# A ViT block of three attentions and a routed feed forward network: half 0 of the data placed ahead of half 1, and the up weights prepared on other engines

## The chip, the cores and the metric

The kernel runs on one core of a Trainium2 chip. The metric is the device time of one execution in microseconds (us); lower is better. The time before is the median of three runs.

A core has five engines that run in parallel, each in order of its own queue: TensorE (PE in the profile; PEld is its loading of weights) multiplies matrices into the eight banks of PSUM, VectorE (DVE) and ScalarE (ACT) compute elementwise from the buffer or from PSUM, GpSimd (POOL) computes elementwise from the buffer alone, and SyncE (SP) issues transfers. They wait for each other on semaphores.

## The reference

The input is 16 images of 3 x 128 x 128. Everything is float32. Cut to what matters here:

```python
h = layer_norm(patches @ conv_w.T + conv_b) + pe           # 16 x 64 tokens, 64 features
identity = h
h = ffn(h)                                                 # gelu, 64 -> 256 -> 64
h = windowed_attention(h) + identity                       # first attention, 8 heads of 8
identity = h
h = ffn(h) + identity                                      # second use of the same ffn: "ffn2"
# second attention: one head of 64, a bias from cosines, inside a block with layer norm
h = layer_norm(h + softmax(q @ k.T / 8 + bias) @ v)
# third: rms norm, rotary q and k, causal attention with 4 heads
x = h + attention(rms_norm(h) * ln1_w) @ wo.T
flat = rms_norm(x) * ln2_w
w = top-2-of-8 softmax(flat @ router_w.T), normalised
y = sum over e of w[e] * (silu(flat @ w1[e].T) * (flat @ w3[e].T)) @ w2[e].T
out = layer_norm(h + x + y)
```

## The kernel before

The 16 images x 64 positions x 64 features lie as 128 partitions x 512 columns (two images' features share the partitions), and nearly every step is done in two halves g = 0 and 1 of 256 columns (`HC`). Each engine's program is one list written out by hand in `build`: the order of the calls is the order of its queue, and semaphores alone tie the engines together. Steps of half 0 and half 1 are interleaved by hand.

What the change touches, in order of time:

- **First attention** (`att1`, L863 and L1269). Eight windows w. TensorE does `scores1(w)`, `turn1(w-1)` (the transpose of the shifted scores), `mix1(w-2)`; VectorE the maximum and the subtraction (`shift`, L1234, L1236); ScalarE the exp (L867). Windows 0 to 3 are half 0. A half ends with `divide` on VectorE (L1245, L1247), `mixed_to_features` on TensorE (two transposes, L426), `attended_copy1` on ScalarE (L861), `project1` on TensorE (L431) and `residual1` on VectorE (L1291), which makes h2.
- **Second feed forward** (`ffn2`): `ffn_up` (L351), two `gelus` on ScalarE (L808), `ffn_down` (L361), `ffn2_out` on VectorE (L1301), which makes h3.
- **Second attention** (`att2`): `queries_keys2` (L500) in two banks that both halves use in turn, q copied by ScalarE (L890), k by VectorE (`keys2`, L1308), `open_scores2` (the bias put in the scores' bank ahead of them, L483), `scores2` (L515), `shift2` on VectorE (L1322, L1324), `turn2` (L506), exp (L896), `values2` (L523 and L1329; the value weights are centred once by `centre_values2`, L1158 and L1165), `mix2` (L536), `divide2` (L1344, L1346), `residual2` (L1351).
- **Root mean square norm**: squares (VectorE L1361 for half 0, ScalarE L903 for half 1), their sums (L1174), ScalarE's square root (L906), reciprocal (L1180) and scaling (L1185) on VectorE, which makes `h4n`; `turn_h4` (L566) and ScalarE's copy `h4f` (L911); then two pairs of products for keys and queries of each half (`turned_pair`, L575), which VectorE rotates (L1375, L1382).
- **The up weights** `up_w` (2816 columns, loaded early) are multiplied by `ln2` and split in a rounded high part `up_hi` and a rest `up_lo`: L1284 and L1296, on VectorE. They are read in the last stage (L707, L708), behind the third attention. `down_w` is centred by GpSimd (L1077 to L1085), which waits for VectorE's key slots (`k1_dve`, L1217) before it starts.

ScalarE has one function table at a time: `bring_table` (L794) loads the next, 1.28 us plus a first use.

## Time and profile before

| | |
|---|---|
| Time, median of 3 runs | 115.91 us (115.75 to 115.92) |
| The profiled execution | 115.73 us, of which its span 113.9 us |
| Mean granted TensorE clock | 0.983 |
| TensorE busy | 100.1 us, 88% |
| VectorE busy | 81.2 us, 71% |
| ScalarE busy | 64.0 us, 56% (nine table loads, 11.5 us) |
| GpSimd busy | 33.3 us, 29% |
| Chain that ended last | TensorE 59%, VectorE 19%, ScalarE 7%, transfers 6% |

The busy shares are averages over stages with different limits. In the first attention (about 21 to 39 us) and in the last stage with the experts' products (73 to 105 us) TensorE is all but full. Between them, from 39 to 72 us, the work passes from engine to engine in two halves, and the chain of waits tells more than the shares. GpSimd's total includes 22.7 us without work, from 32 to 55 us.

### The profile page before, as it was taken

The numbers are of one execution on the slowest core, as the hardware profiler recorded it, in microseconds if no ns is written. First come the engines' busy times: TensorE is split into PE (matmuls) and PEld (weight loads), VectorE is DVE, ScalarE is ACT, GpSimd is POOL, SyncE is SP. The second block draws the span as 40 slices with busy tenths as digits, with TensorE's granted clock in tenths as the row PEclk, the third lists the DMA queues.
The fourth block names the chain that finished last, engine by engine and source line by source line (L and its number), as shares of the span: only waits on it lengthen the run. The fifth ranks groups of instructions, "written<-read, shape, count | busy, mean of one in ns | idle before, by whom it ended". The sixth has DMA issues, their size and how long they took to land.

```text
span 113.9 us, 2196 instructions
## 1 busy us (share of the span) xinstructions
PE 100.1 (88%) x825; PEld 64.5 (57%) x828; DVE 81.2 (71%) x173; ACT 64.0 (56%) x125; POOL 33.3 (29%) x68
## 2 busy tenths in 40 slices
PE   5998979999999998977699887999999999999710
PEld 2334547376676764663568665688888874334400
DVE  0002417597889889889598975589589899976981
ACT  5005364976533754927388657467476667478040
POOL 7500034973830000000622073030012350879000
PEclk9999999999999999999999999999999999999985
DMA  3999994000000000000000000000000000000004
GB/s 125 368 387 419 441 409 172 0 0 0 6 0 0 0 3 6 3 0 0 0 0 6 0 0 6 0 0 0 0 0 6 3 0 0 3 0 0 0 0 92
DMA packets 2826, 6.99 MB, mean 61 GB/s; under 512 B 1280, under 2 KB 1408, under 8 KB 2688
## 3 DMA queue, kind: packets, MB, share of 16 engines
q1 hardware_dynamic: 2272, 6.72, 15.2%
q10 hardware_dynamic: 544, 0.13, 0.5%
q8 instruction: 6, 0.10, 0.4%
q14 instruction: 4, 0.03, 0.1%
HBM read 6.59 MB, written 0.26 MB: 60 GB/s over the span
## 4 chain that ended last, share of the span: by engine, by line
PE 59%; DVE 19%; ACT 7%; DMA 6%; issue 3%; SPq 2%; POOL 1%; DVEq 0%; ACTq 0%
PE PS L707 9%; PE PS L708 9%; PE PS L715 7%; DMA shared_x<-x_dram 6%; PE PS L393 4%; PE PS L351 4%; PE PS L575 3%; PE PS L404 3%; PE PS L361 3%; DVE shifted L1236 2%; DVE top L1234 2%; PE PS L418 2%; ACT shared_f L808 2%; PE PS L327 2%; PE PS L515 1%
## 5 line engine op out<-in xcount | busy, mean ns | idle before, releaser
L707 PE MATMUL PS<-xf,up_hi 128*128 128x512 f32 x44 | 17.8, 405 | 0.2 <-DVE xf L1402 0.2
L1454 DVE TENSOR_TENSOR shared_h<-PS,shared_f 128x512 f32<-128x512 f32 x22 | 15.0, 683 | 3.4 <-ACT shared_f L973 3.1
L708 PE MATMUL PS<-xf,up_lo 128*128 128x512 f32 x44 | 17.3, 394 | 0.0
L973 ACT ACTIVATE shared_f<-PS 128x512 f32<-128x512 f32 x22 | 13.1, 596 | 6.4 <-PE PS L708 6.2
L794 ACT ACT_TABLE_LOAD x9 | 11.5, 1283 | 0.9 <-PEq L1671 0.7
L1234 DVE TENSOR_REDUCE top<-PS 128x8 f32<-128x512 f32 x12 | 8.3, 688 | 3.0 <-PE PS L393 2.7
L707 PEld LDWEIGHTS PS<-xf,up_hi 128*128 128x128 f32 x44 | 8.3, 188 | 2.2 <-issue 0.4
L708 PEld LDWEIGHTS PS<-xf,up_lo 128*128 128x128 f32 x44 | 8.3, 188 | 1.8
L1236 DVE TENSOR_TENSOR shifted<-PS,top 128x512 f32<-128x512 f32 x12 | 8.3, 691 | 0.4
L867 ACT ACTIVATE probs<-PS 128x512 f32<-128x512 f32 x8 | 4.8, 598 | 5.6 <-PE PS L404 5.6
L808 ACT ACTIVATE shared_f<-PS,pack_b_sb 128x512 f32<-128x512 f32 x8 | 5.2, 685 | 4.7 <-PE PS L351 4.6
L715 PE MATMUL PS<-shared_h,down_w 128*64 128x512 f32 x32 | 7.7, 605 | 0.0
L1088 POOL TENSOR_SCALAR std<-sq_sums 128x8 f32<-128x8 f32 x1 | 0.2, 203 | 22.7 <-DVE sq_sums L1174 22.7
L327 PE MATMUL PS<-shared_x 128*64 128x256 f32 x48 | 6.7, 394 | 0.1
L309 PE MATMUL PS<-idle_bf 128*128 128x512 bf16 (+1 forms) x14 | 5.3, 488 | 1.5 <-POOL idle_bf L1016 1.3
L1530 DVE TENSOR_TENSOR shared_x<-PS,up_w 128x512 f32<-128x512 f32 x8 | 5.2, 686 | 1.5 <-PE PS L715 1.1
L1252 DVE TENSOR_SCALAR pos_b<-pack_a_sb 128x64 f32<-128x64 f32 x1 | 0.3, 253 | 8.2 <-DMA pack_a_sb<-pack_a_dram 8.2
L393 PE MATMUL PS<-shared_h,q_groups 64*128 64x256 f32 x32 | 5.6, 427 | 0.2 <-ACT shared_h L841 0.2
L999 ACT ACTIVATE up_w<-PS 128x512 f32<-128x512 f32 x8 | 4.2, 599 | 2.7 <-PE PS L729 2.7
L361 PE MATMUL PS<-shared_f,pack_b_sb 128*64 128x256 f32 x32 | 5.0, 405 | 0.6 <-ACT shared_f L808 0.6
L1142 POOL TENSOR_TENSOR shared_x<-shared_x 128x512 f32<-128x512 f32 x4 | 5.1, 1276 | 1.4 <-DVE shared_x L1530 1.4
L404 PE MATMUL PS<-pack_a_sb,shifted 128*128 128x128 f32 x32 | 5.2, 286 | 0.2 <-ACT q_groups L835 0.2
(206 smaller groups left out, 206.7 us busy)
## 6 DMA issues: line engine op xcount, KB each, us to landing
shared_x<-x_dram SPq DMA_DIRECT2D x3, 512.0 KB, 7.2
up_w<-pack_d_dram SPq DMA_DIRECT2D x1, 1408.0 KB, 11.2
shared_x<-x_dram SPq DMA_DIRECT2D x2, 576.0 KB, 4.0
pack_c_sb<-pack_c_dram SPq DMA_DIRECT2D x1, 796.5 KB, 12.7
shared_x<-x_last_dram SPq DMA_DIRECT2D x2, 288.0 KB, 5.4
pack_b_sb<-pack_b_dram SPq DMA_DIRECT2D x1, 455.0 KB, 8.5
down_w<-pack_e_dram SPq DMA_DIRECT2D x1, 352.0 KB, 13.1
pack_a_sb<-pack_a_dram SPq DMA_DIRECT2D x1, 162.0 KB, 5.6
```

The source lines that it names most:

```text
L327: m = mm(PS[HALF * s:HALF * s + HALF, 4 + g, 0:HC], weights, pixels, start=(n == 0 and k == 0), stop=(last and k == 1))
L361: t = mm(PS[r, bank, 0:HC], b("ff2")[:, m * D:(m + 1) * D], hidden[:, m, s, g * HC:(g + 1) * HC], start=(m == 0), stop=(m == 1))
L393: t = mm(PS[:, SCORE_BANKS[w % 2] + s, 0:HC], q_groups[r, w ^ s].rearrange("q h n -> q (h n)"), k_slots[r, w ^ s].rearrange("q h n -> q (h ...
L404: t = tp(PS[:, w % 2, ch * P:(ch + 1) * P], shifted[:, w % 2, ch * P:(ch + 1) * P], ident)
L707: mm(up, up_hi[:, at:at + P], moving, start=True, stop=False)
L708: mm(up, up_lo[:, at:at + P], moving, start=False, stop=True).then_inc(sem("up_mm"), 1)
L715: t = mm(PS[HALF * s:HALF * s + HALF, bank, tok], down_w[:, DOWN_AT[ch]:DOWN_AT[ch] + D], hh[:, ch, s, tok], start=True, stop=True)
L794: f(table_use[:, :], const(1.0), func)
L973: f(gate[:, n % UPBUF, :], PS[:, UP_BANKS[n % UPBUF][0], :], ACT.Silu).then_inc(sem("gated"), 1)
L1234: v.reduce_max(tops, rows, AX).then_inc(sem(name + "_top"), 1)
L1236: v.tensor_tensor(shifted[:, n % 2, :].rearrange("q (b h n) -> q b h n", b=2, n=N), rows, tops.unsqueeze(3).to_broadcast([P, 2, 4, N]), AL ...
L1454: v.tensor_tensor(hh[:, ch, :, g * HC:(g + 1) * HC], PS[:, UP_BANKS[n % UPBUF][1], :].rearrange("q (s c) -> q s c", s=2), gate[:, n % UPBU ...
```

## The change

It moves work in time and between engines; what is computed stays.

- **Banks.** Half 0 and half 1 get banks of their own between the first attention's end and h3, by five new tuples (`FFN2_UP_BANKS`, `FFN2_BANKS`, `BACK1_BANKS`, `PROJECT_AT`; half 0's transposes and its projection lie in the two halves of bank 4, whose mixes have been divided by then).
- **Half 0 first.** On every engine half 0's steps go ahead of half 1's: its division behind the sixth window, its transposes, projection and up products inside the attention's tail, its down products ahead of half 1's projection. In the second attention half 0's turn, mix, division and residual go ahead of half 1's scores and shift.
- **Weights.** VectorE no longer touches the up weights. GpSimd multiplies `up_w` in place in three pieces of 1024, 896 and 896 columns; ScalarE copies each piece, rounded, to `up_hi` behind windows 3, 4 and 6; GpSimd subtracts each piece to `up_lo`, behind `down_w`.
- **One root.** For half 0's root mean square GpSimd computes the power -0.5 of the mean square (`std_rms` to `rstd_rms`, 4 columns); ScalarE's root and the reciprocal remain for half 1. ScalarE computes both halves' squares.
- **Third attention's start.** Both pairs of products of half 0 go ahead of half 1's turn; the second waits for `ln1_in` 2, since half 1's sum reads the banks it writes. The openings of the third attention's scores are spread among the steps, and one of two idle products goes.

```diff
@@ -271,6 +271,11 @@
 TURNED2_BANKS = (0, 1)
...
 FFN1_BANKS = (6, 1)
+FFN2_UP_BANKS = (6, 2)
+FFN2_BANKS = (4, 7)
+BACK1_BANKS = (4, 1)
+PROJECT_AT = ((4, HC), (3, 0))
+UP_PIECES = (0, 8 * P, 15 * P, 2 * CH * P)
...
 block = ctx.enter_context(nc.Block())
@@ -427,8 +432,9 @@
         t.then_inc(sem(name + "_back"), 1)
...
     def project1(g):
+        bank, at = PROJECT_AT[g]
         pe.wait_ge(sem("att1_ready"), g + 1)
-        mm(PS[:, 2 + g, 0:HC], b("proj"), half(attended, g),
+        mm(PS[:, bank, at:at + HC], b("proj"), half(attended, g),
...
     pe.wait_ge(sem("set_up"), 1)
@@ -470,13 +476,11 @@
     turn1(1)
     for w in range(3, W8):
         scores1(w)
+        if w == W8 - 1:
+            mixed_to_features("att1", BACK1_BANKS[0], 0)
         turn1(w - 1)
         mix1(w - 2)
-    pe.wait_ge(sem("att1_probs"), W8 - 1)
-    mixed_to_features("att1", 0, 0)
-    turn1(W8 - 1)
-    mix1(W8 - 2)
-    mix1(W8 - 1)
     def open_scores2(g):
...
         for n in range(2):
@@ -484,14 +488,15 @@
     project1(0)
+    turn1(W8 - 1)
+    mix1(W8 - 2)
+    ffn_up("ffn2", h2, FFN2_UP_BANKS, 0)
+    mix1(W8 - 1)
     pe.wait_ge(sem("bias_step"), 4)
     open_scores2(0)
-    mixed_to_features("att1", 1, 1)
-    ffn_up("ffn2", h2, (4, 2), 0)
+    mixed_to_features("att1", BACK1_BANKS[1], 1)
+    ffn_down("ffn2", 0, FFN2_BANKS[0])
     project1(1)
-    open_scores2(1)
-    ffn_down("ffn2", 0, 6)
-    ffn_up("ffn2", h2, (4, 2), 1)
...
     def queries_keys2(g):
         pe.wait_ge(sem("h3_ready"), g + 1)
@@ -543,23 +548,25 @@
     pe.wait_ge(sem("pack_c_loaded"), 16)
     queries_keys2(0)
-    ffn_down("ffn2", 1, 7)
+    open_scores2(1)
+    ffn_up("ffn2", h2, FFN2_UP_BANKS, 1)
     scores2(0)
-    queries_keys2(1)
+    ffn_down("ffn2", 1, FFN2_BANKS[1])
+    turn2(0)
     pe.wait_ge(sem("v2_centred"), 2)
     values2(0)
-    turn2(0)
-    scores2(1)
+    queries_keys2(1)
     mix2(0)
-    values2(1)
-    turn2(1)
-    mix2(1)
     pe.wait_ge(sem("masks_made"), 2)
     open_scores3(0)
+    values2(1)
+    scores2(1)
+    open_scores3(2)
+    turn2(1)
+    open_scores3(3)
+    mix2(1)
+    stay_awake(1, 1)
     open_scores3(1)
-    open_scores3(2)
-    stay_awake(2, 5)
-    open_scores3(3)
     def turn_h4(g):
         pe.wait_ge(sem("h4n_ready"), g + 1)
         for u in (2 * g, 2 * g + 1):
@@ -577,8 +584,9 @@
     turn_h4(0)
     turned_pair(0, ("fk", "fk_turned"))
+    pe.wait_ge(sem("ln1_in"), 2)
+    turned_pair(0, ("fq", "fq_turned"))
     turn_h4(1)
-    turned_pair(0, ("fq", "fq_turned"))
     pe.wait_ge(sem("rope_k"), 1)
     turned_pair(1, ("fk", "fk_turned"))
     pe.wait_ge(sem("rope_q"), 1)
@@ -682,7 +690,7 @@
         pe.wait_ge(sem("xf_ready0"), g + 1)
         pe.wait_ge(sem("xf_ready1"), g + 1)
...
-    pe.wait_ge(sem("up_split"), 2)
+    pe.wait_ge(sem("up_split"), 3)
     half_ready(0)
     for n in range(2 * CH):
         g, ch = n // CH, n % CH
@@ -858,7 +866,12 @@
     def attended_copy1(g):
         act.wait_ge(sem("att1_back"), g + 1)
-        f(half(attended, g), PS[:, g, 0:HC], ACT.Copy).then_inc(sem("att1_ready"), 1)
+        f(half(attended, g), PS[:, BACK1_BANKS[g], 0:HC], ACT.Copy).then_inc(sem("att1_ready"), 1)
+    def up_high(n):
+        piece = slice(UP_PIECES[n], UP_PIECES[n + 1])
+        act.wait_ge(sem("up_scaled"), n + 1)
+        f(up_hi[:, piece], up_w[:, piece], ACT.Copy).then_inc(sem("up_high"), 1)
...
     for w in range(W8):
         act.wait_ge(sem("att1_turned"), w + 1)
@@ -873,42 +886,51 @@
             last_slot1(1)
         if w == 2:
             values1(1)
+        if w in (3, 4):
+            up_high(w - 3)
+        if w == W8 - 3:
+            attended_copy1(0)
         if w == W8 - 2:
-            attended_copy1(0)
-    bring_table(ACT.Gelu_apprx_tanh)
-    attended_copy1(1)
-    for g in range(2):
-        gelus("ffn2", (4, 2), g)
-    act.wait_ge(sem("q2_bias_made"), 1)
-    for g in range(2):
+            up_high(2)
+    def queries2(g):
         act.wait_ge(sem("qk2_mm"), g + 1)
         for s in range(2):
             r = slice(HALF * s, HALF * s + HALF)
...
         t.then_inc(sem("q2_act"), 1)
-        if g == 0:
-            bring_table(ACT.Exp)
-    for g in range(2):
+    def probabilities2(g):
         act.wait_ge(sem("att2_turned"), g + 1)
...
           ACT.Exp).then_inc(sem("att2_probs"), 1)
...
-    bring_table(ACT.Sqrt)
-    for g in range(2):
-        if g == 1:
-            act.wait_ge(sem("ln1_in"), 2)
-            f(half(squares, 1), half(sum2, 1), ACT.Square).then_inc(sem("ln1_squared"), 1)
-        at = slice(4 * g, 4 * g + 4)
-        act.wait_ge(sem("ln1_sq_sum"), g + 1)
-        f(std_rms[:, at], sq_sums[:, at], ACT.Sqrt, scale=(1.0 + EPS_RMS) / D, bias=const(EPS_RMS * EPS))\
-            .then_inc(sem("rms1_std"), 1)
-    for g in range(2):
+    def squares1(g):
+        act.wait_ge(sem("ln1_in"), g + 1)
+        f(half(squares, g), half(sum2, g), ACT.Square).then_inc(sem("ln1_squared"), 1)
+    def features_copy(g):
         act.wait_ge(sem("h4_turned"), g + 1)
...
+    bring_table(ACT.Gelu_apprx_tanh)
+    gelus("ffn2", FFN2_UP_BANKS, 0)
+    attended_copy1(1)
+    act.wait_ge(sem("q2_bias_made"), 1)
+    queries2(0)
+    gelus("ffn2", FFN2_UP_BANKS, 1)
+    bring_table(ACT.Exp)
+    probabilities2(0)
+    queries2(1)
+    squares1(0)
+    probabilities2(1)
+    bring_table(ACT.Sqrt)
+    features_copy(0)
+    squares1(1)
+    act.wait_ge(sem("ln1_sq_sum"), 2)
+    f(std_rms[:, 4:8], sq_sums[:, 4:8], ACT.Sqrt, scale=(1.0 + EPS_RMS) / D, bias=const(EPS_RMS * EPS))\
+        .then_inc(sem("rms1_std"), 1)
+    features_copy(1)
     for g in range(2):
         act.wait_ge(sem("kr_ready"), g + 1)
         for h in range(2):
@@ -1065,6 +1087,10 @@
     pool.wait_ge(sem("bias_step"), 3)
...
+    pool.wait_ge(sem("up_w_loaded"), 16)
+    for n in range(3):
+        piece = up_w[:, UP_PIECES[n]:UP_PIECES[n + 1]]
+        g_.tensor_scalar(piece, piece, a("ln2"), None, ALU.mult).then_inc(sem("up_scaled"), 1)
@@ -1084,9 +1110,19 @@
     pool.wait_ge(sem("down_summed"), 7)
...
+    for n in range(3):
+        piece = slice(UP_PIECES[n], UP_PIECES[n + 1])
+        pool.wait_ge(sem("up_scaled"), n + 1)
+        pool.wait_ge(sem("up_high"), n + 1)
+        g_.tensor_tensor(up_lo[:, piece], up_w[:, piece], up_hi[:, piece].bitcast(F32), ALU.subtract).then_inc(sem("up_split"), 1)
+    pool.wait_ge(sem("ln1_sq_sum"), 1)
+    g_.tensor_scalar(std_rms[:, 0:4], sq_sums[:, 0:4], (1.0 + EPS_RMS) / D, EPS_RMS * EPS, ALU.mult, ALU.add).then_inc(sem("variance"), 1)
+    pool.wait_ge(sem("variance"), 2)
+    g_.tensor_tensor(rstd_rms[:, 0:4], std_rms[:, 0:4], minus_half[:, 0:4], ALU.pow).then_inc(sem("rms1_rstd"), 1)
     pool.wait_ge(sem("ln1_sq_sum"), 2)
...
-    pool.wait_ge(sem("variance"), 2)
+    pool.wait_ge(sem("variance"), 3)
...
     for g in range(2):
         pool.wait_ge(sem("rope_q"), g + 1)
@@ -1278,27 +1314,18 @@
             first_slots1(1, range(3))
         if w == 3:
             values1(1)
-        if w == 6:
+        if w == 5:
             divide("att1", 4, 0, HEADS, HD)
-    ve.wait_ge(sem("up_w_loaded"), 16)
-    v.tensor_scalar(up_hi[:, :], up_w[:, :], a("ln2"), None, ALU.mult).then_inc(sem("up_high"), 1)
-    divide("att1", 5, 1, HEADS, HD)
-    ve.wait_ge(sem("biases_made"), 2)
-    ve.wait_ge(sem("up_high"), 1)
...
     def residual1(g):
+        bank, at = PROJECT_AT[g]
         ve.wait_ge(sem("proj_mm"), g + 1)
-        v.scalar_tensor_tensor(out=half(h2, g), in0=PS[:, 2 + g, 0:HC], scalar=proj_bias[:, 0:1],
+        v.scalar_tensor_tensor(out=half(h2, g), in0=PS[:, bank, at:at + HC], scalar=proj_bias[:, 0:1],
...
-    def up_low(g):
-        up = slice(g * CH * P, (g + 1) * CH * P)
-        v.scalar_tensor_tensor(out=up_lo[:, up], in0=up_w[:, up], scalar=a("ln2"), in1=up_hi[:, up].bitcast(F32),
-                               op0=ALU.mult, op1=ALU.subtract).then_inc(sem("up_split"), 1)
...
     def ffn2_out(g):
         ve.wait_ge(sem("ffn2_down"), g + 1)
-        v.scalar_tensor_tensor(out=half(h3, g), in0=PS[:, 6 + g, 0:HC], scalar=b("ff2_b"),
+        v.scalar_tensor_tensor(out=half(h3, g), in0=PS[:, FFN2_BANKS[g], 0:HC], scalar=b("ff2_b"),
...
     def keys2(g):
@@ -1308,13 +1335,13 @@
         t.then_inc(sem("k2_dve"), 1)
...
+    ve.wait_ge(sem("biases_made"), 2)
     residual1(0)
-    up_low(0)
-    residual1(1)
     ve.wait_ge(sem("pack_c_loaded"), 16)
     centre_values2()
+    divide("att1", 5, 1, HEADS, HD)
     ffn2_out(0)
-    up_low(1)
+    residual1(1)
     def shift2(g):
         ts = slice(4 * g, 4 * g + 4)
@@ -1330,11 +1357,10 @@
     keys2(0)
+    shift2(0)
     ffn2_out(1)
-    shift2(0)
+    values2(0)
     keys2(1)
-    values2(0)
-    shift2(1)
...
     def divide2(g):
         ts = slice(4 * g, 4 * g + 4)
@@ -1351,18 +1377,19 @@
     def normalised1(g):
-        invert("rms1", g, rstd_rms, std_rms)
+        if g == 1:
+            ve.wait_ge(sem("rms1_std"), 1)
+            v.reciprocal(rstd_rms[:, 4:8], std_rms[:, 4:8]).then_inc(sem("rms1_rstd"), 1)
...
     divide2(0)
+    residual2(0)
+    shift2(1)
+    sum_squares("ln1", 0)
     values2(1)
-    residual2(0)
-    ve.wait_ge(sem("ln1_in"), 1)
-    v.tensor_tensor(half(squares, 0), half(sum2, 0), half(sum2, 0), ALU.mult).then_inc(sem("ln1_squared"), 1)
-    sum_squares("ln1", 0)
+    normalised1(0)
     divide2(1)
     residual2(1)
-    normalised1(0)
     sum_squares("ln1", 1)
     normalised1(1)
```

TensorE, from the scores of window 7 on. Before (L393 scores, L404 turn, L418 mix, L426 transposes of a half, L431 projection, L483 opening of scores2, L351 up products):

```order
L393 MATMUL PS<-shared_h,q_groups 128x256 x2
L404 MATMUL PS<-pack_a_sb,shifted 128x128 x4
L418 MATMUL PS<-vo,probs 64x18 x8
L426 MATMUL PS<-pack_a_sb,s2 128x128 x2
L404 MATMUL PS<-pack_a_sb,shifted 128x128 x4
L418 MATMUL PS<-vo,probs 64x18 x16
L431 MATMUL PS<-attended,pack_b_sb 128x256
L483 MATMUL PS<-bias_parts,ident_r 128x256 x2
L426 MATMUL PS<-pack_a_sb,s2 128x128 x2
L351 MATMUL PS<-h2,pack_b_sb 128x256 x4
L431 MATMUL PS<-attended,pack_b_sb 128x256
```

The same place now (the lines in the same order: L398, L409, L423, L431, L437, L487, L356, and L366 the down products):

```order
L398 MATMUL PS<-shared_h,q_groups 128x256 x2
L431 MATMUL PS<-pack_a_sb,s2 128x128 x2
L409 MATMUL PS<-pack_a_sb,shifted 128x128 x4
L423 MATMUL PS<-vo,probs 64x18 x8
L437 MATMUL PS<-attended,pack_b_sb 128x256
L409 MATMUL PS<-pack_a_sb,shifted 128x128 x4
L423 MATMUL PS<-vo,probs 64x18 x8
L356 MATMUL PS<-h2,pack_b_sb 128x256 x4
L423 MATMUL PS<-vo,probs 64x18 x8
L487 MATMUL PS<-bias_parts,ident_r 128x256 x2
L431 MATMUL PS<-pack_a_sb,s2 128x128 x2
L366 MATMUL PS<-shared_f,pack_b_sb 64x256 x4
```

Half 0's transposes moved ahead of two turns, its projection ahead of the last turn, its up products ahead of the last mix; its down products now follow half 1's transposes directly.

VectorE, from half 0's division on. Before (L1284 and L1296 are the up weights):

```order
L1245 RECIPROCAL r1<-PS 128x32
L1247 TENSOR_TENSOR s2<-PS,r1 128x256
L1234 TENSOR_REDUCE top<-PS 128x8
L1236 TENSOR_TENSOR shifted<-PS,top 128x512
L1284 TENSOR_SCALAR up_hi<-up_w,pack_a_sb 128x2816
L1245 RECIPROCAL r1<-PS 128x32
L1247 TENSOR_TENSOR s2<-PS,r1 128x256
L1291 SCALAR_TENSOR_TENSOR h2<-PS,proj_bias,h0 128x256
L1296 SCALAR_TENSOR_TENSOR up_lo<-up_w,pack_a_sb,up_hi 128x1408
L1291 SCALAR_TENSOR_TENSOR h2<-PS,proj_bias,h0 128x256
```

And now (L1281, L1283 division; L1194, L1201 centring of the value weights):

```order
L1281 RECIPROCAL r1<-PS 128x32
L1283 TENSOR_TENSOR s2<-PS,r1 128x256
L1270 TENSOR_REDUCE top<-PS 128x8
L1272 TENSOR_TENSOR shifted<-PS,top 128x512
L1270 TENSOR_REDUCE top<-PS 128x8
L1272 TENSOR_TENSOR shifted<-PS,top 128x512
L1323 SCALAR_TENSOR_TENSOR h2<-PS,proj_bias,h0 128x256
L1194 TENSOR_REDUCE means<-pack_c_sb 128x2
L1201 SCALAR_TENSOR_TENSOR pack_c_sb<-means,pack_c_sb 128x128
L1194 TENSOR_REDUCE means<-pack_c_sb 128x1
L1201 SCALAR_TENSOR_TENSOR pack_c_sb<-means,pack_c_sb 128x64
L1281 RECIPROCAL r1<-PS 128x32
```

The division moved ahead by one window, the passes over the weights are gone, and the centring stands between the two halves' steps.

VectorE at the second attention's end. Before, from half 0's division:

```order
L1344 RECIPROCAL r2<-PS 128x4
L1346 TENSOR_TENSOR attended<-PS,r2 128x256
L1329 TENSOR_TENSOR v2<-PS,pack_c_sb 128x4x64
L1351 TENSOR_TENSOR h2<-PS,attended 128x256
L1361 TENSOR_TENSOR squares<-h2 128x256
L1174 TENSOR_REDUCE sq_sums<-squares 128x4
L1344 RECIPROCAL r2<-PS 128x4
L1346 TENSOR_TENSOR attended<-PS,r2 128x256
L1351 TENSOR_TENSOR h2<-PS,attended 128x256
L1180 RECIPROCAL rstd_rms<-std_rms 128x4
L1185 TENSOR_TENSOR kf<-h2,rstd_rms 128x256
```

And now:

```order
L1370 RECIPROCAL r2<-PS 128x4
L1372 TENSOR_TENSOR attended<-PS,r2 128x256
L1377 TENSOR_TENSOR h2<-PS,attended 128x256
L1349 TENSOR_REDUCE s2_top<-PS 128x4
L1351 TENSOR_TENSOR s2_shift<-PS,s2_top 128x256
L1210 TENSOR_REDUCE sq_sums<-squares 128x4
L1356 TENSOR_TENSOR v2<-PS,pack_c_sb 128x4x64
L1221 TENSOR_TENSOR kf<-h2,rstd_rms 128x256
L1370 RECIPROCAL r2<-PS 128x4
L1372 TENSOR_TENSOR attended<-PS,r2 128x256
L1377 TENSOR_TENSOR h2<-PS,attended 128x256
```

Half 1's maximum and subtraction (L1349, L1351) moved behind half 0's sum, the multiplication to squares is gone, and half 0's scaling (L1221), which waits for GpSimd's power, now stands ahead of half 1's division.

## Rows read from the trace of the kernel before

**Rows 1.** Chain of waits, 54 to 60 us: start, length in us, engine, line.
```profile
54.05 0.43 DVE kf L1185
...
54.87 0.30 ACT std_rms L906
...
55.58 1.13 PE PS L575 x4
56.71 0.22 PE PS L566 x2
56.93 2.78 PE PS L575 x12
```

**Rows 2.** Timeline of TensorE: start, length in us, line, out<-in, count [idle before].
```profile
36.18 0.44 PE L426 MATMUL PS<-pack_a_sb,s 128*128 128x128 f32 x2
...
38.60 0.70 PE L431 MATMUL PS<-attended,pack_b_sb 128*128 128x256 f32 x2
...
39.98 1.14 PE L351 MATMUL PS<-h,pack_b_sb 64*128 64x256 f32 x8
...
46.44 0.68 PE L515 MATMUL PS<-k,qf 64*64 64x64 f32 x16 [0.23 <-ACT qf L890]
...
49.20 0.68 PE L515 MATMUL PS<-k,qf 64*64 64x64 f32 x16 [0.64 <-DVE k L1308]
```

**Rows 3.** Timeline of VectorE, 26 to 61 us.
```profile
26.37 0.88 DVE L1217 TENSOR_SCALAR shared_h<-kf,pack_b_sb 128x256 f32<-128x256 f32 x3
27.77 0.69 DVE L1234 TENSOR_REDUCE top<-PS 128x8 f32<-128x512 f32 x1 [0.52 <-PE PS L393]
...
36.54 1.68 DVE L1284 TENSOR_SCALAR up_hi<-up_w,pack_a_sb 128x2816 fp32r<-128x2816 f32 x1
...
43.21 0.47 DVE L1301 SCALAR_TENSOR_TENSOR h<-PS,pack_b_sb,h 128x256 f32<-128x256 f32 x1
43.61 1.67 DVE L1296 SCALAR_TENSOR_TENSOR up_lo<-up_w,pack_a_sb,up_hi 128x1408 fp32r<-128x1408 f32 x1
...
53.51 0.43 DVE L1351 TENSOR_TENSOR h<-PS,attended 128x256 f32<-128x256 f32 x1
...
55.41 0.42 DVE L1185 TENSOR_TENSOR kf<-h,rstd_rms 128x256 f32<-128x256 f32 x1
...
60.81 0.69 DVE L1234 TENSOR_REDUCE top<-PS 128x8 f32<-128x512 f32 x1 [0.33 <-PE PS L596]
```

**Rows 4.** Timeline of ScalarE, 33 to 42 us.
```profile
33.74 0.60 ACT L867 ACTIVATE probs<-PS 128x512 f32<-128x512 f32 x1 [1.20 <-PE PS L404]
...
37.99 1.28 ACT L794 ACT_TABLE_LOAD   x1
...
41.16 1.27 ACT L808 ACTIVATE shared_f<-PS,pack_b_sb 128x512 f32<-128x512 f32 x2 [0.71 <-PE PS L351]
```

**Rows 5.** Timeline of GpSimd, 16 to 33 us.
```profile
16.40 1.03 POOL L1043 TENSOR_TENSOR rstd<-std,minus_half 128x4 f32<-128x4 f32 x1
...
21.14 0.90 POOL L1060 TENSOR_SCALAR pack_c_sb<-pack_c_sb 128x64 f32<-128x64 f32 x2
...
23.84 1.05 POOL L1070 CAST pick<-pack_c_sb 128x1024 fp32r<-128x1024 f32 x1
27.40 0.93 POOL L1077 TENSOR_TENSOR route_parts<-down_w 128x352 f32<-128x352 f32 x1 [2.51 <-DVE shared_h L1217]
...
30.83 1.39 POOL L1085 TENSOR_TENSOR down_w<-down_w,route_parts 128x704 f32<-128x704 f32 x1
```

**Rows 6.** Timeline of all engines at 18.8 us, GpSimd and VectorE.
```profile
18.80 0.47 POOL L1047 TENSOR_SCALAR router_s<-pack_c_sb,pack_a_sb 128x8 f32<-128x8 f32 x1 [1.37 <-DMA pack_c_sb<-pack_c_dram]
...
18.88 0.87 DVE L1217 TENSOR_SCALAR shared_h<-kf,pack_b_sb 128x256 f32<-128x256 f32 x3
```

**Rows 7.** Timelines of VectorE and of GpSimd at 105 us.
```profile
105.51 0.71 DVE L1533 TENSOR_TENSOR s<-shared_x 128x512 f32<-128x512 f32 x1
...
103.16 2.51 POOL L1142 TENSOR_TENSOR shared_x<-shared_x 128x512 f32<-128x512 f32 x2
```

## The prediction, made before the result was known

> **What bounds the kernel now.** I read the chain of waits first, in the stretch that the change touches, then the timeline of each engine there. No single engine is full between 41 and 60 us: the chain changes engine every half microsecond. It ends with one half of the data queued behind the other on TensorE [rows 1]. Half 0 is normalised on VectorE at 54.05, its copy reaches TensorE at 55.58, and the products of half 0 (1.13 us for the first pair) stand in front of half 1's turn, which starts at 56.7 though half 1's normalised rows were ready at 55.83 [rows 1, 3]. From 56.93 on TensorE runs the last three pairs of products back to back for 2.78 us, and the third attention's first maximum starts at 60.81 [rows 1, 3]. The reader is to see that half 0 comes too late to use the gap while half 1 is still being worked on.
>
> Why half 0 is late stands in the same views. VectorE spends 1.68 us on the high parts of the up weights at 36.54 and two times 1.67 us on the low parts [rows 3]; TensorE issues the projection of half 0 only at 38.60, behind the last turn and two mixes [rows 2]; ScalarE's gelus of half 0 start at 41.16, though their table is in at 39.5 (load 37.99 plus 1.28 plus 0.2 for its first use) [rows 4]; the output of the second feed forward network of half 0 starts at 43.21 [rows 3]. In the first attention itself TensorE is the bound: ScalarE idles 1.20 us before each exp [rows 4].
>
> **The change, part by part.** All times are from the start of the profiled span. I take each instruction's duration from its row or from the same line's other rows, start it when its data and its engine are both free, and compare with where it started before. I did this working for before too, and it comes within 0.2 us of the trace everywhere, so differences are better than absolute times.
>
> *First attention's end.* VectorE's division of half 0 goes ahead of the seventh window's maximum. Its mixes are done at 32.5, so it runs 32.8 to 33.6 and costs that maximum 0.4 us, which TensorE doesn't feel: two transposes of half 0, 0.44 us long [rows 2], now stand in front of the seventh turn. That turn comes 0.4 us later, the eighth by 0.05. Half 0's projection is issued at 36.4 instead of 38.60, its residual is done at 37.6, and the up products start at 37.9 instead of 39.98 [rows 2]. The last mix pays: it is pushed from 38.06 to 38.96 by 0.9 us, and with it everything of half 1.
>
> *The weights.* VectorE loses 1.68 + 2 x 1.67 = 5.0 us [rows 3]. GpSimd takes a multiplication and a subtraction of 2816 columns, ScalarE the rounding copies. No GpSimd row is a multiplication of this size. Its copy of 1024 columns takes 1.05 us, and multiplications by a per-partition scalar of 64 columns 0.45 us each [rows 5]; 512 columns with two inputs take 1.26 to 1.28 (2.51 for two) [rows 7]. So the three multiplications cost between 2.9 us (the copy's rate) and 7.0 us (the two-input rate); I take 3.7 us, the copy's rate plus 0.25 us for each, as it is nearest in form: one input. They would run from 23.1 to 26.9. The three subtractions go by the two-input rate, 2816 x 2.5 ns = 7.0 us at most, 6.5 us with a fixed part taken off. GpSimd has room: it is idle from 32.2 to 54.9 [rows 5], so they run from 33.9 to about 40.4, and the first reader is the up product behind the third attention. ScalarE's copies: 512 columns of exp take 0.60 us [rows 4], so 1024 take at most 1.20, 896 at most 1.05. Two of them lie in gaps of 1.20 us; the third, behind the seventh exp, ends at 37.5, just as the last turn does. I cost them at nothing on the path, and at most at 0.1 us for the third. If the cover is gone, each microsecond of them delays an exp by as much.
>
> *Feed forward network and second attention, half 0.* The gelu table is in at 39.55, so the gelus start there instead of at 41.16: 1.6 us earlier. Part is given back: the down products stand behind the transposes of half 1, which wait for the division behind the last mix (38.96, then 39.65 to 40.45). They start at 40.85, and half 0's output starts at 42.07 instead of 43.21, 1.15 us earlier. Queries and keys are ready at 44.15, the scores start at 44.6 instead of 46.44 [rows 2] since half 1's down products no longer stand in front. From there the exp table binds: it now waits for both halves' gelus and is in at 47.5. The exps of half 0 start then; in my working of before they start 1.4 us later, behind the turn. The sum of half 0 is ready at 50.1, its squares are summed at 51.4 behind half 1's shift.
>
> *One root on GpSimd.* The power of 4 columns takes 1.03 us [rows 5], and the multiplication in front of it 0.2 to 0.3 with its wait: 51.4 to 52.7. ScalarE's table load for the root no longer matters to half 0, and its rows are normalised at 52.8 instead of 54.05 [rows 1]: 1.25 us earlier.
>
> *Half 1.* It pays the 0.9 us of the last mix; gaps in front of its gelus and its scores take back most. Its scores start at 49.4, 0.2 later than the 49.20 of before [rows 2]. Then VectorE, which runs in order, waits with the second division until half 0 is normalised, a wait that the change adds: behind it stand the division, the sum and the squares of half 1, and ScalarE's root. The sum comes at 53.7 instead of 53.51 [rows 3], and the normalised rows of half 1 at 55.6 to 56.0 instead of 55.41 to 55.83 [rows 3], 0.2 to 0.3 us later.
>
> *Where the gain is cashed.* Half 0's copy is at TensorE at 54.15, so its two pairs of products run 54.15 to 56.0, before half 1 arrives. Half 1's turn starts at 56.0 instead of 56.7 [rows 1], its copy ends at 56.9, its first pair starts at 57.0 instead of 57.6, and the third attention's scores start at 58.7 instead of 59.6. The first maximum of the third attention starts at 59.9 against 60.81 [rows 3] (against 60.65 in my working of before): 0.8 us, the smaller of the two. Behind that nothing is changed, and VectorE and TensorE alternate there with no long wait that could give the time back. The clock is granted in full in the touched stretch (PEclk digits of 9), and TensorE's gaps there stay below 1 us, as they are now, so I price the clock at nothing.
>
> So the profiled time is 115.73 - 0.8 = 114.9 us, of which 1.8 lie outside the span; the median of the shown runs is 0.18 higher, and against it the forecast is 115.91 - 0.8 = 115.1 us. Within 0.2%, 0.23 us, is about what a measurement can't tell from no change.
>
> **The port that VectorE and GpSimd share.** The change lets long GpSimd instructions run beside VectorE at two places. The first is at 26.37, where VectorE copies half 1's key slots, three multiplications from buffer to buffer in 0.88 us [rows 3]; GpSimd was idle from 24.9 to 27.40 there [rows 5], and is now in the third multiplication and the pick copies until about 28.8. The only overlap of this kind in the trace is at 18.8: GpSimd's multiplication of 8 columns is in flight from 18.80 to 19.27, and the same three VectorE instructions start at 18.88 and take 0.87 us, no longer than without it [rows 6]. With 8 columns that says little about 896. The second is the centring of the value weights, about 37.6, with two buffer inputs, beside the subtractions. At 105.51 VectorE starts a sum with two buffer inputs while GpSimd's last sum is in flight until 105.67, and takes 0.71 us, 0.02 above its sister [rows 7]. The sum above goes by these rows: no delay.
> The Trainium skill, page "SBUF — State Buffer", section "Who interferes with whom", says otherwise: a VectorE instruction in a two-port mode or with two inputs in the buffer and a GpSimd instruction that reads the buffer exclude each other, and the second to issue waits for the whole of the first. By that rule the small overlaps of rows 6 and 7 should show a delay of up to 0.4 and 0.16 us, and they show 0.0 and 0.02; no row has a long overlap, so it is a rival with a chance of its own.
>
> **The rivals.**
> *A, slower: VectorE's key slots are held up by GpSimd at 26.4.* Price: if each of the three instructions waits for a GpSimd instruction of its own (what is left of the third multiplication, 0.5 us; 0.75; 1.05), they end 2.35 us later. VectorE idles 0.52 us before its next maximum [rows 3], and TensorE is by my working 0.3 us from needing what follows it, so 0.8 us are free; each further microsecond delays the whole loop, which TensorE bounds. At worst 1.55 us are lost: 115.9 - 0.8 + 1.55 = 116.7. It decides from a hold of 1.6 us on, where the gain is gone; with one instruction held, 0.5 us, nothing is lost. For: the overlap is certain. Against: rows 6.
> *B: the centring is held up by the subtractions at 37.9.* Two instructions, the first until 38.3, the second until 40.4: centring ends at 40.6 instead of 38.6. It has 1.0 us before the second division, so 1.0 us is lost to half 1's transposes and the down products behind them: 115.9 - 0.8 + 1.0 = 116.1.
> *C: half 1 sets the end and half 0's lead is worth nothing.* Half 1 is 0.2 to 0.3 us later by my sum, and every further 0.1 us in its path (the added wait for the power, the last mix) costs 0.1 at the end. If the wait for the power is 0.6 us longer than I have it, because GpSimd starts late or half 0's squares do, the time is 115.7; with 0.8, 115.9, no change. For: VectorE's queue has the division behind the wait, and the sums before it leave no slack. Against: rows 5 have the power at 1.03 us.
>
> **How the numbers follow.** Forecast 0.58, at 115.1. A 0.15 at 116.0 to 116.7, B 0.10 at 116.1, C 0.17 at 115.7 to 115.9. Faster takes the forecast and 0.07 of C: 0.65. Same takes 0.10 of C and half of B: 0.15. Slower is A and the rest of B: 0.20. The range reaches up to 116.3, which takes in C, B and the cheaper part of A and leaves some 0.1 of A out. Down, if the added wait for the power is hidden, 0.3 us more are gained, and 0.2 us is what my working errs by: 115.9 - 0.8 - 0.5 = 114.6.
>
> **What would show it.** In the profile after: the up products of half 0 at 37.9, its gelus at 39.6, its output addition at 42.1, half 0 normalised at 52.8, half 1 at 55.6, TensorE doing both pairs of half 0 before half 1's turn, and the first maximum of the third attention at 59.9. A shows as key slots of VectorE that take well over 0.35 us each, and a fourth maximum after 27.8; B as centring instructions of over 0.5 us at 38; C as a gap before half 0's scaling on VectorE longer than 1.2 us. I am wrong on ScalarE's copies if an exp starts late in the fifth or sixth window, and wrong on the end if half 1's turn doesn't start when its rows are ready.

## The result

The change makes the kernel slower: 120.42 us median (119.89 to 121.69, four runs) against 115.91 us, a ratio of 1.038 with a 95% interval of 1.033 to 1.043. The forecast was 115.1 us. The profiled execution took 119.91 us, its span 118.1 us, at a mean granted clock of 0.972. A median here is over all executions of a kernel; its ratio and interval leave out those that lie more than 1.5% above the kernel's fastest.

Since the first attention starts at another moment in each profile (21.27 us before, 21.48 after, 21.03 to 22.18 in the experiments), I measure from its first maximum to the third attention's first maximum, "the stretch" below, and from there to the end of the span, "the tail". The stretch grew from 39.54 us (60.81 in [rows 3] less 21.27) to 43.25, the tail from 53.09 to 53.37 (spans are read to 0.1 us, so a tail is good to about 0.05).

VectorE's timeline of the changed kernel, at the place where [rows 3] have the division and the weights (start, length in us, line, operation, out<-in, count, idle before and who ended it):

```profile
37.95 2.11 DVE L1201 SCALAR_TENSOR_TENSOR pack_c_sb<-means,pack_c_sb 128x128 f32<-128x128 f32 x1
40.09 0.22 DVE L1194 TENSOR_REDUCE means<-pack_c_sb 128x1 f32<-128x64 f32 x1
40.34 1.73 DVE L1201 SCALAR_TENSOR_TENSOR pack_c_sb<-means,pack_c_sb 128x64 f32<-128x64 f32 x1
41.99 0.34 DVE L1281 RECIPROCAL r<-PS 128x32 f32<-128x32 f32 x1
...
45.24 0.48 DVE L1328 SCALAR_TENSOR_TENSOR h<-PS,pack_b_sb,h 128x256 f32<-128x256 f32 x1 [2.45 <-PE PS L366]
```

GpSimd's timeline, the multiplications and the subtractions of the up weights:

```profile
23.18 7.86 POOL L1093 TENSOR_SCALAR up_w<-up_w,pack_a_sb 128x1024 f32<-128x1024 f32 x3
...
37.55 6.48 POOL L1117 TENSOR_TENSOR up_lo<-up_w,up_hi 128x1024 fp32r<-128x1024 f32 x3
```

The two centring instructions L1201 took 2.11 and 1.73 us; in the profile before the same two took 0.29 and 0.23. Both began while a subtraction of GpSimd was in flight (the three end at 39.91, 41.99 and 44.03), and both ended within 0.15 us of a subtraction's end, at 40.05 and 42.07. The reduction between them, which reads one buffer, took its usual 0.22. VectorE runs in order, so half 1's division waited to 41.99 and TensorE, whose next work is that division's transpose, stood still:

```profile
39.71 0.50 PE L487 MATMUL PS<-bias_parts,ident_r 128*128 128x256 f32 x2
42.85 0.44 PE L431 MATMUL PS<-pack_a_sb,s 128*128 128x128 f32 x2 [2.63 <-DVE s L1283]
43.22 1.98 PE L366 MATMUL PS<-shared_f,pack_b_sb 128*64 128x256 f32 x8
```

The gap was followed by a lower clock. The windows of the changed kernel (stretch, its length, busy time and instructions of PE, PEld, DVE, ACT, POOL, then the granted clock, DMA share, GB/s):

```profile
38.00:40.00 2.00, 2.00 (x32) 1.57 (x28) 2.00 (x1) 1.97 (x4) 2.00 (x2) 1.00 0.01 4
40.00:42.00 2.00, 0.22 (x2) 0.01 (x1) 1.93 (x4) 0.87 (x2) 2.00 (x2) 1.00 0.00 0
42.00:44.00 2.00, 1.15 (x6) 0.74 (x8) 0.76 (x3) 0.38 (x1) 2.00 (x1) 0.81 0.00 0
44.00:46.00 2.00, 2.00 (x8) 0.74 (x4) 0.48 (x1) 0.00 (x0) 0.03 (x1) 0.50 0.00 0
46.00:48.00 2.00, 2.00 (x11) 1.23 (x12) 1.27 (x3) 0.73 (x2) 0.00 (x0) 0.83 0.03 8
```

TensorE was busy for 0.22 us between 40 and 42; from 44 to 46 it was granted 0.50, that is 1.2 GHz. Half 0's eight down products took 1.98 us; in the profile before, at full clock, the same eight took 1.23. What stands behind is late as well: the output of the feed forward network of half 0 starts at 45.24 instead of 43.21 before, the third attention's first maximum at 64.73 instead of 60.81. How much of this is the hold's and how much the clock's, experiments 1 and 2 tell apart.

### The profile page after: what moved, and what is told of

Read it like the earlier page. It is cut to its first block, busy times and chain, and to the rows that moved or that the text cites. A ratio compares the mean times of both kernels' runs of the same rounds, so it can differ in the third digit from the quotient of the medians.

```text
span 118.1 us, 2206 instructions
## 1 busy us (share of the span) xinstructions
PE 102.8 (87%) x827; PEld 65.3 (55%) x827; DVE 79.9 (68%) x168; ACT 66.9 (57%) x128; POOL 48.8 (41%) x76
## 4 chain that ended last, share of the span: by engine, by line
PE 71%; DVE 16%; ACT 7%; issue 3%; POOL 1%; DVEq 0%; ACTq 0%; POOLq 0%
PE PS L715 9%; PE PS L716 9%; PE PS L723 6%; PE PS L398 4%; PE PS L366 4%; PE PS L332 4%; PE PS L314 4%; PE PS L409 3%; PE PS L582 3%; DVE pack_c_sb L1201 3%; PE PS L356 3%; PE PS L423 2%; ACT shared_f L816 2%; PE PS L437 2%; DVE shifted L1272 1%
## 5 line engine op out<-in xcount | busy, mean ns | idle before, releaser
L1093 POOL TENSOR_SCALAR up_w<-up_w,pack_a_sb 128x896 f32<-128x896 f32 (+1 forms) x3 | 7.9, 2631 | 0.0
L1117 POOL TENSOR_TENSOR up_lo<-up_w,up_hi 128x896 fp32r<-128x896 f32 (+1 forms) x3 | 6.5, 2188 | 0.0
L366 PE MATMUL PS<-shared_f,pack_b_sb 128*64 128x256 f32 x32 | 5.7, 465 | 0.5 <-ACT shared_f L816 0.4
L398 PE MATMUL PS<-shared_h,q_groups 64*128 64x256 f32 x32 | 5.6, 427 | 0.2 <-ACT shared_h L849 0.2
```

The source lines that it names most:

```text
L366: t = mm(PS[r, bank, 0:HC], b("ff2")[:, m * D:(m + 1) * D], hidden[:, m, s, g * HC:(g + 1) * HC], start=(m == 0), stop=(m == 1))
L398: t = mm(PS[:, SCORE_BANKS[w % 2] + s, 0:HC], q_groups[r, w ^ s].rearrange("q h n -> q (h n)"), k_slots[r, w ^ s].rearrange("q h n -> q (h ...
```

## The experiments

The theory after the first look: (H) VectorE's centring is held by GpSimd's subtractions; (K) the gap that this makes costs a second time by the clock. The rivals: the subtractions or the new order cost something else; and, for what would be left after H and K, that half 1 sets the end (C of the prediction). A result is given as a median with its ratio to the kernel before, run beside it on the same chip.

**1. The subtractions wait for the centring** (on the changed kernel):

```diff
+            pool.wait_ge(sem("v2_centred"), 2)
             for n in range(3):
                 piece = slice(UP_PIECES[n], UP_PIECES[n + 1])
```

> The changed kernel, but GpSimd waits for the second part of VectorE's centring of the value weights before it starts its three subtractions; nothing is left out. Theory H (hold): the two centring instructions with two buffer inputs (2.11 and 1.73 us where they took 0.29 and 0.23) were held by GpSimd's subtractions, and TensorE's gap of 2.63 us and its lower clock behind it come from that alone. Then both take 0.2 to 0.3 us again, the granted clock stays 1.00 from 42 to 48 us, the first maximum of the third attention comes at 60.1 (59.9 plus the 0.2 by which the changed kernel was late at 21 us), and the time is the forecast: 114.8 to 115.6. Rival U (order): the order of half 0 ahead of half 1 costs the time, since TensorE's down products stand behind transposes that wait for VectorE; then a gap over 1.5 us stays in front of the transposes and the time is 118 or more. Between them, 116 to 117.5: GpSimd's slow multiplications (2.84 and 2.5 us each, where 1.3 and 1.2 were forecast) also cost.

Measured: 116.41 us, ratio 1.004 (1.001 to 1.007). VectorE's timeline:

```profile
37.50 0.29 DVE L1202 SCALAR_TENSOR_TENSOR pack_c_sb<-means,pack_c_sb 128x128 f32<-128x128 f32 x1
37.83 0.22 DVE L1195 TENSOR_REDUCE means<-pack_c_sb 128x1 f32<-128x64 f32 x1
38.08 0.23 DVE L1202 SCALAR_TENSOR_TENSOR pack_c_sb<-means,pack_c_sb 128x64 f32<-128x64 f32 x1
39.38 0.36 DVE L1282 RECIPROCAL r<-PS 128x32 f32<-128x32 f32 x1 [1.07 <-PE PS L423]
```

The hold, the gap and the low clock are gone, and with them 3.62 us of the stretch (39.63). But the time is above the expected 114.8 to 115.6 us, and the stretch is not the 38.7 of the forecast; it is that of the kernel before. So H and K are most of the result, and 0.8 us of forecast gain are missing for another reason. It isn't GpSimd's slow multiplications, the third branch of the expectation: they stay as slow in experiment 9, which gets the 0.8 us back.

**2. The gap filled.** On the changed kernel, ten idle products before the transposes of half 1; they change nothing that is computed.

```diff
             open_scores2(0)
+            stay_awake(10, 3)
             mixed_to_features("att1", BACK1_BANKS[1], 1)
```

> The changed kernel with ten idle products of 512 columns (0.22 us each) in TensorE's queue in front of half 1's transposes, so in its gap; GpSimd and VectorE are as in the changed kernel, nothing is left out. It splits the loss in the hold and the clock. Theory H: centring stays at about 4.4 us, the granted clock stays 1.00 from 42 to 48 us, the down products of half 0 take 1.2 us instead of 1.98 and the time falls by 1.5 to 2.2 us to 118.2 to 118.9. Rival: the clock falls for another reason than the gap; then it is at 0.5 from 44 to 46 us here too and the time stays at 120.4.

Measured: 118.75 us, ratio 1.024 (1.021 to 1.027). TensorE's timeline, and the window behind it:

```profile
40.77 2.10 PE L314 MATMUL PS<-idle_bf 128*128 128x512 bf16 x9
43.12 0.44 PE L431 MATMUL PS<-pack_a_sb,s 128*128 128x128 f32 x2 [0.24 <-DVE s L1284]
43.49 1.08 PE L366 MATMUL PS<-shared_f,pack_b_sb 128*64 128x256 f32 x8
```

```profile
44.00:46.00 2.00, 1.95 (x13) 0.86 (x10) 0.97 (x3) 0.00 (x0) 0.30 (x1) 1.00 0.00 0
```

Nine of the ten idle products stand in the trace; a matmul record can be missing. The centring is held as before (1.87 and 1.75 us), the clock stays at 1.00, and the down products take 1.08 instead of 1.98. The stretch is 41.57. So of the 3.71 us that the stretch grew, 43.25 - 41.57 = 1.68 are the clock's, 41.57 - 39.63 = 1.94 the hold's, and 0.09 remain. The hold was 0.2 us shorter here than in the changed kernel, whose second division starts 20.51 us behind the first maximum against 18.35 without a hold; by that profile the split is 2.16 and 1.46.

**3. The weights alone.** The kernel before, with only the weights moved to GpSimd and ScalarE (copies behind windows 3, 4 and 5), and the wait of experiment 1.

```diff
+            pool.wait_ge(sem("up_w_loaded"), 16)
+            for n in range(3):
+                piece = up_w[:, UP_PIECES[n]:UP_PIECES[n + 1]]
+                g_.tensor_scalar(piece, piece, a("ln2"), None, ALU.mult).then_inc(sem("up_scaled"), 1)
...
-            v.tensor_scalar(up_hi[:, :], up_w[:, :], a("ln2"), None, ALU.mult).then_inc(sem("up_high"), 1)
...
-            up_low(0)
...
-            up_low(1)
```

> The kernel before with one part of the change alone: the up weights are multiplied and subtracted by GpSimd and copied by ScalarE (behind windows 3, 4 and 5), with the subtractions behind VectorE's centring so that they can't hold it; the order of the halves, the banks and the root are those of before; nothing is left out. If the gain of the guarded change is from the order, this gives 115.5 to 116.0 (freeing VectorE of 5.0 us moves half 1's division from 38.72 to 38.7, as TensorE's last mix sets it, and its keys by nothing); if it is from VectorE's free time, this gives 115.1.

Measured: 116.58 us, ratio 1.005 (1.002 to 1.008). Both expectations missed. The stretch is 39.51, as before: five microseconds less on VectorE are worth nothing in the old order. Most of the cost lies in the tail, 53.48 instead of 53.09. VectorE and GpSimd there, to be read beside [rows 7]:

```profile
105.40 1.07 DVE L1542 TENSOR_TENSOR s<-shared_x 128x512 f32<-128x512 f32 x1
...
102.06 3.85 POOL L1161 TENSOR_TENSOR shared_x<-shared_x 128x512 f32<-128x512 f32 x3 [0.77 <-DVE shared_x L1539]
```

GpSimd ends at 102.06 + 3.85 = 105.91, VectorE at 105.40 + 1.07 = 106.47: 0.56 later. In experiment 1 the same sum took 0.97 and ended 0.56 behind GpSimd. In [rows 7] GpSimd ends at 105.67 and VectorE at 106.22: 0.55 later. One rule fits all three: a held sum does about 0.14 us of its own 0.69 first, and the other 0.55 behind GpSimd's end. By it an overlap of 0.16 us, as in [rows 7], shows as 0.02. The row that I had read as "no delay" looks the same with a hold as without one, so it says nothing against a hold.

**4. The hold by itself.** The kernel before, with a tail behind its output in which VectorE starts an instruction of 256 columns 0.14 to 0.19 us into one of GpSimd of 1024. The tail is added work, and the kernel was run once.

```diff
+                if kind == 0:
+                    t = g_.tensor_tensor(shared_h[:, 2048:3072], shared_h[:, 0:1024], shared_h[:, 2048:3072], ALU.add)
+                elif kind == 1:
+                    t = g_.tensor_scalar(shared_h[:, 2048:3072], shared_h[:, 0:1024], a("ln2"), None, ALU.mult)
```

> The kernel before with a tail of twenty small measurements behind its last normalisation, so its time is longer and says nothing; its outputs are the kernel's. Each measurement starts a GpSimd instruction of 1024 columns (four kinds: two inputs; multiplication by a per-partition scalar; copy; multiplication by a constant) and, some 0.4 us into it, one VectorE instruction of 256 columns (five kinds: two buffer inputs; per-partition multiplication buffer to buffer; one PSUM and one buffer input; reduction from the buffer; copy buffer to buffer). Theory H: with two buffer inputs VectorE is held to GpSimd's end beside the two-input kind (about 2 us instead of 0.42); with one buffer input or PSUM it takes its 0.42 to 0.48 us always. If the hold is by any GpSimd instruction for its whole length, the key slots' form (multiplication buffer to buffer) takes 2 us beside the per-partition multiplication; the changed kernel's 0.58 us for the first of three says it is held for less than that. If the port doesn't matter at all and something else stretched the centring, every form takes its usual time.

VectorE's rows beside GpSimd's sum with two inputs, beside its multiplication by a per-partition scalar, and the GpSimd rows:

```profile
112.71 2.45 DVE L1586 TENSOR_TENSOR h<-h 128x256 f32<-128x256 f32 x1
...
115.66 2.32 DVE L1588 TENSOR_SCALAR h<-h,pack_a_sb 128x256 f32<-128x256 f32 x1
...
126.53 1.25 DVE L1586 TENSOR_TENSOR h<-h 128x256 f32<-128x256 f32 x1
...
129.68 1.11 DVE L1588 TENSOR_SCALAR h<-h,pack_a_sb 128x256 f32<-128x256 f32 x1
...
112.54 2.34 POOL L1157 TENSOR_TENSOR shared_h<-shared_h 128x1024 f32<-128x1024 f32 x1 [6.08 <-DVE r L1582]
...
126.39 2.85 POOL L1159 TENSOR_SCALAR shared_h<-shared_h,pack_a_sb 128x1024 f32<-128x1024 f32 x1 [0.51 <-DVE r L1582]
```

Beside the sum, everything of VectorE from buffer to buffer but a reduction is held to the end: 2.45, 2.32 and, for a copy, 2.32. I had expected that of two buffer inputs only. A product of PSUM and buffer and a reduction took 0.41 each, unheld, like the reduction in the changed kernel. Beside GpSimd's multiplication the same instructions were held for about 0.8 us of its 2.85 only. The multiplication itself is the slower instruction, 2.85 us for 1024 columns against 2.34 with two inputs.

Not every instruction of GpSimd with two inputs holds VectorE. In the kernel before, GpSimd computes a power for 1.68 us:

```profile
55.28 1.68 POOL L1090 TENSOR_TENSOR rstd<-std,minus_half 128x8 f32<-128x8 f32 x1
```

Half 1's scaling on VectorE, with both inputs in the buffer, starts 0.13 us into it (55.41, [rows 3]) and takes 0.42 us; half 0's, with GpSimd idle, took 0.43. The changed kernel has the same at 60.09 (0.43). So the hold is shown for sums, subtractions and copies that read hundreds of columns, in part for multiplications, and not for this power of 8 columns.

**5. The centring early.** The changed kernel, centring ahead of the first window, no added wait on GpSimd:

```diff
             first_slots1(0, range(3))
+            ve.wait_ge(sem("pack_c_loaded"), 16)
+            centre_values2()
...
             residual1(0)
-            ve.wait_ge(sem("pack_c_loaded"), 16)
-            centre_values2()
```

> The changed kernel with the centring of the value weights moved, on VectorE, ahead of the first attention's first maximum, where GpSimd has no long instruction in flight; the subtractions are not held back by anything. Hold theory: both centring instructions at their length of before (0.29 and 0.23 us), subtractions free to start at 37.5, TensorE's gap at 40 below 0.6 us, clock in full, and the time of the kernel with the guard, 116.4 us (116.1 to 116.7), 4 us under the changed kernel. If it was GpSimd's subtractions themselves (their traffic beside TensorE and ScalarE), not the centring, that slowed the changed kernel, this one stays at 119 or more.

Measured: 116.55 us, ratio 1.003 (0.999 to 1.008); the stretch is 39.63, that of experiment 1 to the hundredth, with the subtractions free to run from 37.24. So the subtractions cost the stretch nothing but through what they hold.

**6. Half 1's path.** On experiment 1, two steps of TensorE moved:

```diff
             queries_keys2(0)
-            open_scores2(1)
             ffn_up("ffn2", h2, FFN2_UP_BANKS, 1)
...
             mix2(0)
+            open_scores2(1)
+            scores2(1)
             pe.wait_ge(sem("masks_made"), 2)
             open_scores3(0)
             values2(1)
-            scores2(1)
```

> The kernel with the guard, with two steps of TensorE in another place: the bias for half 1's scores is opened behind the mixing of half 0 instead of ahead of half 1's up products, and half 1's scores go ahead of its values. Theory that half 1's path sets the end (rival C): half 1's up products start 0.35 us earlier, its scores at 49.0 to 49.3 instead of 49.72, its sum and its normalised rows 0.3 to 0.5 us earlier (normalised at 55.6 instead of 56.02), the third attention's first maximum at 60.2 to 60.4 instead of 60.66, time 115.9 to 116.1 us. Theory that half 0's lead sets the end: only half 0's own changes count, its scores come 0.2 earlier at most, and the time stays at 116.3 to 116.5.

Measured: 115.61 us, ratio 0.997 (0.9938 to 0.9995): a little faster than the kernel before, and below the expected 115.9 to 116.1. Half 1 is normalised 34.70 us behind the first maximum instead of 34.99, half 0 at 31.79 instead of 32.07. The profile shows a loss as well, of 0.58 us, at the key slots; VectorE's timeline:

```profile
27.19 2.04 DVE L1254 TENSOR_SCALAR shared_h<-kf,pack_b_sb 128x256 f32<-128x256 f32 x3
29.16 0.68 DVE L1271 TENSOR_REDUCE top<-PS 128x8 f32<-128x512 f32 x1
```

In the changed kernel and in experiments 1, 2, 3, 5 and 7 these three took 0.88 to 1.16 us, and the fourth maximum came 6.50 us behind the first, as in the kernel before; here it is 7.08. Rival A is real, but not in every execution: the multiplications start at 22.46 here and the slots at 27.19, 1.90 us into the second multiplication's 2.53; in experiment 1 they start 3.41 us behind GpSimd and lose 0.2, with 3.6 to 3.8 us between them they lose nothing.

**7. Smaller pieces.** The changed kernel, each subtraction in two instructions:

```diff
+                middle = (piece.start + piece.stop) // 2
+                for part in (slice(piece.start, middle), slice(middle, piece.stop)):
+                    t = g_.tensor_tensor(up_lo[:, part], up_w[:, part], up_hi[:, part].bitcast(F32), ALU.subtract)
+                t.then_inc(sem("up_split"), 1)
```

> The changed kernel with each of GpSimd's three subtractions cut into two instructions of half the columns (1.1 to 1.25 us each); no guard. If a centring instruction is held to the end of the one GpSimd instruction in flight, the two are held 1.3 us at most each instead of 1.8 and 1.5 (sum of delays 0.8 to 2.0 us instead of 3.4), the gap of TensorE at 40 falls to 0.9 to 1.9 us, and the time to 117 to 118.8. If VectorE were shut out for as long as GpSimd has such work queued, the centring would end with the last subtraction as before or later, and the time stay at 120 or more.

Measured: 116.67 us, ratio 1.005 (1.002 to 1.007), with GpSimd in such work all the while. VectorE's timeline:

```profile
38.47 0.71 DVE L1204 SCALAR_TENSOR_TENSOR pack_c_sb<-means,pack_c_sb 128x128 f32<-128x128 f32 x1
...
39.47 0.92 DVE L1204 SCALAR_TENSOR_TENSOR pack_c_sb<-means,pack_c_sb 128x64 f32<-128x64 f32 x1
40.35 0.36 DVE L1284 RECIPROCAL r<-PS 128x32 f32<-128x32 f32 x1
```

The delays add up to 1.11 us, as expected: an instruction is held to the end of the one instruction in flight, not for as long as GpSimd has work. The time is below the expected 117 to 118.8, since I had forgotten that the second division has 1.07 us to spare (the idle time in experiment 1): a hold of 1.1 us is free, and there is no gap for the clock. The stretch is 39.63, the same as with no hold at all.

**8. Experiments 5 and 6 together** (no wait on GpSimd):

> The early centring and the two moved steps of TensorE together, on the changed kernel, without the guard. If both accounts hold, as the kernel with the guard and the moved steps: 115.9 to 116.1 us, and no centring held. If the subtractions cost anything to VectorE's other work between 37.5 and 44 (its residuals and the division read TensorE's buffers in part), it is 0.2 to 0.5 us slower than that kernel.

Measured: 116.12 us, ratio 1.000 (0.996 to 1.003). The profile has the key slots at 2.37 us and the fourth maximum 7.39 behind the first, which is 0.89 us lost, and a stretch of 39.66. The median is 0.51 us above experiment 6's, the size that the expectation gives if the subtractions cost more. The profiles say otherwise: less the loss at the key slots, the stretch is 38.77 here and 38.76 in experiment 6 (39.34 - 0.58). What else moves the median is open.

**9. The key slots kept free.** On experiment 6:

```diff
                 piece = up_w[:, UP_PIECES[n]:UP_PIECES[n + 1]]
+                if n == 1:
+                    pool.wait_ge(sem("k1_dve"), 6)
```

> The kernel with the guard and the moved steps, with one more wait: GpSimd's second and third multiplication wait until VectorE has written the key slots of half 1. Theory that rival A is alive in part of the executions (the key slots took 2.04 and 2.37 us in two profiles and 0.88 to 1.16 in the others, by where they fell in GpSimd's multiplication): key slots 0.88 us in every profile, fourth maximum 6.5 us behind the first, and the median 0.2 to 0.5 us under 115.61, so 115.1 to 115.4. Theory that the spread has nothing to do with the key slots: the median stays at 115.5 to 115.7. The later end of GpSimd's multiplications (33.5 instead of 30.5) has 3 us of room before the third copy of ScalarE; the second copy may wait 0.1.

Measured: 115.56 us, ratio 0.995 (0.992 to 0.998). Key slots 0.88, fourth maximum 6.51 behind the first, stretch 38.85. The median is hardly lower than in experiment 6, against the 115.1 to 115.4 that I expected. So the profiles show the loss and its end; that it moves the median is not shown. `down_w`'s centring by GpSimd is later now and holds the first centring for 1.30 us, inside the spare time.

**10. The tail.** On experiment 9, the sums of the experts' products in another order, meant to have GpSimd done before VectorE's first sum of a GpSimd result:

```diff
-            pool.wait_ge(sem("expert_weighted"), 4)
-            sum_pair(2, 3)
-            pool.wait_ge(sem("pairs_summed"), 2)
-            sum_pair(0, 2)
-            pool.wait_ge(sem("expert_weighted"), 6)
-            sum_pair(4, 5)
+            for n in (2, 3, 4):
+                pool.wait_ge(sem("expert_weighted"), n + 1)
+                pool.wait_ge(sem("pairs_summed"), n - 1)
+                sum_pair(0, n)
```

> The kernel before it in this list, with the sums of the experts' products at the end associated in another way: GpSimd adds the products 1 to 4 to product 0 one after the other as they come, instead of 0+1, 2+3, (0+1)+(2+3), 4+5; VectorE adds 6+7, then 5, then GpSimd's sum. GpSimd is then done at 105.0 instead of 105.7, before VectorE's first sum starts at 105.3. If that sum (0.97 and 1.07 us in all kernels with the weights on GpSimd, 0.71 before) was held to the end of GpSimd's last sum, it takes 0.69 to 0.71 us, and the time is 0.25 to 0.3 us lower: 114.8 to 115.1. If the 0.26 us come from something else in the tail, its length stays at 0.97 and the time is unchanged.

Measured: 115.18 us, ratio 0.991 (0.988 to 0.994), the fastest kernel here. The timelines of VectorE and of GpSimd:

```profile
104.89 0.70 DVE L1561 TENSOR_TENSOR s<-shared_x 128x512 f32<-128x512 f32 x1
...
99.48 5.55 POOL L1181 TENSOR_TENSOR shared_x<-shared_x 128x512 f32<-128x512 f32 x4 [0.94 <-DVE shared_x L1558]
```

The sum took 0.70 where experiment 9's took 0.97, and the tail fell by about 0.3, from 53.45 to 53.12. GpSimd wasn't quite done: it ends at 105.03, 0.14 us into the sum, which by the rule of experiment 3 costs nothing. Why GpSimd's last sums come later in all kernels with the weights on it is open: VectorE's product before them started 0.22 us later in experiment 1 than in the kernel before, counted from the third attention's first maximum, with no releaser in the trace.

**11. The weights alone, with the key wait** (experiment 3 plus the wait of experiment 9):

> The kernel before with only the weights moved (the third experiment), with the same wait between GpSimd's multiplications. If the key slots are what the weights' move costs in part of the executions, the ratio falls from 1.005 to 1.001 to 1.003 (0.3 us remain from the hold in the tail): 116.1 to 116.3 us beside 116.0 for the kernel before. If the cost of 0.5 us is something else (ScalarE's copies, the traffic), the ratio stays at 1.005.

Measured: 116.57 us, ratio 1.003 (1.000 to 1.006). It lies at the edge of what was expected and can't be told from experiment 3. Its stretch is 39.50 and its tail 53.55, with the sum at 1.07 us: in the profiles, what the weights' move costs by itself is the tail.

**12. The root back on ScalarE**, on experiment 10:

```diff
             bring_table(ACT.Sqrt)
+            root(0)
             features_copy(0)
             squares1(1)
...
-            g_.tensor_tensor(rstd_rms[:, 0:4], std_rms[:, 0:4], minus_half[:, 0:4], ALU.pow).then_inc(sem("rms1_rstd"), 1)
```

> The kernel with the guard, the moved steps, the key wait and the reordered tail, with half 0's root taken back from GpSimd to ScalarE's square root, as before the change; VectorE's order is kept. ScalarE's table for the root is in at 53.2 in that kernel's trace, so half 0 is normalised at 53.8 instead of 52.63, and VectorE's second division stands behind it: half 1 is 1.1 us later too, and the time 0.9 to 1.2 us longer, 116.1 to 116.4 us. If the root on GpSimd were worth nothing (VectorE's wait for the power is as long as the wait for the table), the time stays at 115.2.

Measured: 116.95 us, ratio 1.006 (1.003 to 1.009). VectorE waits for ScalarE's table where it waited 1.12 us for the power:

```profile
53.93 0.18 DVE L1218 RECIPROCAL rstd_rms<-std_rms 128x4 f32<-128x4 f32 x1 [1.99 <-ACT std_rms L930]
...
54.62 0.44 PE L573 MATMUL PS<-pack_a_sb,kf 128*128 128x128 f32 x2 [1.06 <-DVE kf L1223]
```

The stretch is 39.94 against 38.84: 1.10 us, as expected. The median differs by more (1.77 us) and lies above the expected 116.1 to 116.4; the executions above 117 us have a mean clock of 0.975 to 0.977, where experiment 10's have 0.985 to 0.993. Whether the added gap of 1.06 us on TensorE brings that clock is not shown.

The kernels side by side, from their profiles:

| | stretch | tail | median | ratio |
|---|---|---|---|---|
| before | 39.54 | 53.09 | 115.91 | |
| the change | 43.25 | 53.37 | 120.42 | 1.038 |
| 2: gap filled | 41.57 | 53.36 | 118.75 | 1.024 |
| 1: hold removed | 39.63 | 53.34 | 116.41 | 1.004 |
| 6: half 1's steps moved | 39.34 | 53.38 | 115.61 | 0.997 |
| 9: key slots free | 38.85 | 53.45 | 115.56 | 0.995 |
| 10: tail sums reordered | 38.84 | 53.12 | 115.18 | 0.991 |
| 12: root back on ScalarE | 39.94 | 53.10 | 116.95 | 1.006 |

## Why the prediction was wrong

**The step that failed is "The sum above goes by these rows: no delay".** The prediction had the hold, as rival B, with its place and its waiting instructions, and gave it 0.10 because rows 6 and 7 showed delays of 0.0 and 0.02 us. In its place the centring was held for 3.32 us. Row 7 was misread: an overlap of 0.16 us can't show a hold, since a held sum does 0.14 us of its own work first. Row 6 stands, but it is beside a multiplication, which holds VectorE only in part. And "no row has a long overlap" was wrong: the power at 55.28 overlaps a scaling of VectorE by the whole of its 0.42 us and doesn't hold it (experiment 4). That row would have spoken against B too; no row of the kernel before has a long GpSimd instruction of the subtractions' kind beside a VectorE instruction from buffer to buffer. Only a run such as experiment 4 could tell beforehand.

The Trainium skill, page "SBUF — State Buffer", section "Who interferes with whom", says that whoever issues second blocks for the whole of the first, and that a VectorE instruction with at most one input in the buffer, outside the two-port modes, and a reduction are free of it. Beside GpSimd's sum and copy the runs agree (2.45 us beside 2.34, 1.13 beside 1.04, and 0.41 for the free ones); beside its multiplication by a scalar they don't (1.25 beside 2.85), nor beside the power (0.42 beside 1.68). The measurement decides.

**The multiplications were mis-sized**: 3.7 us taken, 7.86 measured, beyond even the upper bound of 7.0, which rested on the two-input rate; a one-input instruction turned out slower than a two-input one. As GpSimd's `down_w` work still has to come between, the subtractions stood at 37.55 to 44.03 instead of 33.9 to 40.4. With the forecast size they would have ended at 38.3 and 40.4 around the centring, a hold of 2 us, as B has it; with the true one the centring met the first 0.40 us into its 2.36 and the second 0.48 us into its 2.13.

**The price of B was too small.** I had 1.0 us. The centring was delayed by 2.11 + 1.73 - 0.29 - 0.23 = 3.32 us, of which some 1.1 were spare; 1.94 to 2.16 reached the end. And "TensorE's gaps there stay below 1 us, as they are now, so I price the clock at nothing" holds for the forecast and not for the rival: B's own gap is the reason for another 1.46 to 1.68 us. A rival has to be costed with the gap that it makes.

**The gain was not there either.** With the hold and the gap gone, half 0 is normalised 0.71 us earlier than before, not 1.25, and half 1 0.85 later, not 0.2 (experiment 1: 32.07 and 34.99 behind the first maximum, before 32.78 and 34.14). The step "gaps in front of its gelus and its scores take back most" failed: half 1's up products stood behind the opening of its scores' bank, and its scores behind its values, so that its scores started 28.69 us behind the first maximum instead of 27.93, 0.76 later and not 0.2. That is rival C, by other steps than the two that it names. Moving them gave 0.78 us back (39.63 to 38.85), which is the size of the forecast gain: in experiment 9 half 0 is normalised at 31.30 and half 1 at 34.21 behind the first maximum, where the forecast has 31.5 and 34.3. The end in the tail was taken as unchanged and cost 0.28.

**What held.** In the changed kernel half 0's projection was issued at 36.43 (36.4 forecast), its gelus at 39.6; ScalarE's copies took 1.05 and 0.94 us as priced and delayed no exp; the power on GpSimd with its multiplication took the forecast 1.3 us in experiment 1 (51.75 to 53.07) and is worth 1.10 us by experiment 12. The key slots, rival A, took 0.22 us longer in the changed kernel's profile, which delayed nothing, since the fourth maximum came 6.50 us behind the first as before; in two others it came 0.58 and 0.89 us later, below the 1.55 at worst. A's price has a slip in it: its three waits of 0.5, 0.75 and 1.05 us add up to 2.30, not 2.35. The order of the halves is sound with those two steps moved; the weights' move collided with it.

**The sum.** Of the 3.99 us between the profiles of before and after in stretch and tail, 3.62 are the hold and the clock that followed it (1.94 and 1.68 by experiment 2), 0.28 the tail and 0.09 the rest. Of the remaining 0.5 us of the medians' difference, 0.21 is a later start in this profile; two of the four executions took longer at a mean clock of 0.944 and 0.957, and no trace of them tells why.

## What to carry to other kernels

Work that goes to an idle GpSimd is not free for VectorE: look, for every VectorE instruction from buffer to buffer but a reduction that stands in its time, whether it can wait for one whole GpSimd instruction, and cost that to the end. To read a hold in a trace, find a long overlap beside a GpSimd instruction of the same kind, and compare the end of the second instruction with the end of the first; an overlap of 0.16 us decides nothing, and one beside another kind (the power) can mislead. Guard the few vulnerable instructions with a wait on GpSimd's side, or cut GpSimd's work so that one piece fits in the spare time of what it holds; and price with each rival the gap it makes on TensorE, as the clock may charge it again.

## What the runs showed of the hardware

- GpSimd in float32 from buffer to buffer, 1024 columns, in experiment 4: two inputs 2.34 us, multiplication by a per-partition scalar 2.85, by a constant 2.77, copy 1.04. The one-input arithmetic is slower than the two-input one.
- Beside a copy of GpSimd (1.04 us), VectorE's buffer instructions took 1.00 to 1.13, held to its end; beside the constant multiplication 1.02 to 1.16, as beside the scalar one.
- In GpSimd's multiplication the hold depends on the moment: experiment 4's instructions, 0.15 us into it, lost about 0.8; key slots that came 0.6 us into it lost 0.2, at 0.8 to 1.0 us nothing, at 1.6 and 1.9 us they were held to its end. Why is open.
- Beside GpSimd's power of 8 columns (1.68 us) a VectorE instruction with two inputs in the buffer took 0.42, unheld.
- A gap of 2.63 us on TensorE was followed by some 3.4 us at half clock (granted 0.81, 0.50 and 0.83 in three windows of 2 us), and with products in the gap by none.
